# Moving a weight-tile store to the head of its pump slot, and one pump slot behind the softmax rescale, in an eight-core adaLN transformer layer

## What is computed

```python
h = _layernorm(x) * (1 + ca) + sa
x = x + ga * attn(h)      # k,q,v = h Wk', h Wq', h Wv'; ak = k Wa'
                          # alpha = softmax(q ak'); out = alpha (v Wb')
h = _layernorm(x) * (1 + cb) + sb
x = x + gb * ffn(h)       # two linears with LoRA, exact gelu between
# weights of the ffn:
scale = jnp.max(jnp.abs(w)) / qmax
wq = jnp.clip(jnp.round(w / scale), -qmax - 1, qmax) * scale
```

## Time and profile before

| | us |
|---|---|
| timed runs | 3199.82 and 3276.5, median 3238.16 |
| profiled execution | 3197.74 |
| its slowest core, first to last instruction (the span) | 3196.2 |
| fastest core of the same execution | 3181.2 |
| busy in the span: PE, DVE, ACT, POOL | 1727.2, 1033.1, 763.0, 436.4 |

### The profile page before, as it was taken

The page is one execution under the profiler, slowest core; times in us unless marked ns, Lnnn a source line. Parts: engine busy times, 40 slices in busy tenths (PEclk is TensorE's granted clock), DMA queues, the critical chain, the costliest instruction groups (busy, mean ns, idle before and its releaser), DMA issues.

```text
span 3196.2 us, 24948 instructions; the slowest of 8 cores (3181.2 to 3196.2 us)
## 1 busy us (share of the span) xinstructions
PE 1727.2 (54%) x7994; PEld 764.0 (24%) x7994; DVE 1033.1 (32%) x1773; ACT 763.0 (24%) x1325; POOL 436.4 (14%) x585
## 2 busy tenths in 40 slices
PE   4520040426666555455665555664525858858588
PEld 1110010112222222222232222232212323323233
DVE  3410333434444543444345434345411020110201
ACT  2310001032222231333233333233303122031220
POOL 0001122213333100111111122112200000000000
PEclk9855575758787767777777777777757979979799
DMA  4500424232222210111111222112241113112130
GB/s 141 177 6 5 138 84 132 76 115 70 68 70 69 73 57 30 56 69 70 60 56 66 75 67 69 60 57 70 69 166 53 60 46 99 51 56 65 47 99 27
DMA packets 92297, 233.40 MB, mean 73 GB/s; under 512 B 25380, under 2 KB 25509, under 8 KB 92152
## 3 DMA queue, kind: packets, MB, share of 16 engines
q1 hardware_dynamic: 65000, 160.33, 16.2%
q0 software_dynamic: 27168, 71.47, 6.7%
HBM read 193.85 MB, written 37.88 MB: 73 GB/s over the span
## 4 chain that ended last, share of the span: by engine, by line
PE 33%; DMA 24%; DVE 16%; issue 12%; ACT 10%; POOL 2%; SPq 1%; DVEq 1%; ACTq 0%; POOLq 0%
PE pO L1436 7%; PE pO L1198 5%; PE pE L1394 5%; PE pE L1101 5%; DMA wfcst<-wfcq_sc 4%; DMA amst<-wfc_in 4%; DMA amst<-wpj_in 4%; PE pE L1126 4%; ACT h_stage L729 3%; DVE qkf L960 2%; DMA wm<-wmod_in 2%; DMA q_stg<-q_sc 2%; DMA bfcT_sc<-lora 2%; DVE amx L621 2%; PE pE L742 1%
## 5 line engine op out<-in xcount | busy, mean ns | idle before, releaser
L1394 PE MATMUL pE<-h,wfcst 128*128 128x512 bf16 x1024 | 248.9, 387 | 54.2 <-DMA wfcst<-wfcq_sc 43.8
L936 POOL TENSOR_TENSOR qt<-qt,qkf 128x1024 f32<-128x1024 f32 x64 | 153.4, 2397 | 912.9 <-ACT qkf L930 898.5
L1436 PE MATMUL pO<-wpj_sb,hid 128*128 128x512 bf16 x1024 | 226.3, 379 | 16.1 <-DVE outb L1452 12.4
L1101 PE MATMUL pE<-ak_fm,q_stg 128*128 128x512 bf16 x512 | 144.0, 451 | 136.7 <-DMA q_stg<-q_sc 128.8
L621 DVE TENSOR_REDUCE amx<-amst 128x1 f32<-128x256 f32 x256 | 106.9, 418 | 183.6 <-DMA amst<-wfc_in 91.7
L1198 PE MATMUL pO<-u_tm,alphaT 128*128 128x512 bf16 x512 | 152.8, 472 | 22.0 <-DVE alphaT L1077 22.0
L930 ACT ACTIVATE qkf<-qki 128x512 f32<-128x512 int32 x128 | 80.5, 629 | 316.2 <-DVE qki L927 316.2
L1069 PE MATMUL pT<-idb,alphaA 128*128 128x128 bf16 x256 | 32.1, 305 | 220.7 <-DVE qbf L1011 135.6
L1409 ACT ACTIVATE hid<-pE,bfc_col 128x512 bf16<-128x512 f32 x128 | 88.0, 687 | 232.9 <-PE pE L1402 232.9
L742 PE MATMUL pE<-h_stage,wkaT 128*128 128x512 bf16 x512 | 125.3, 410 | 30.3 <-ACT h_stage L729 30.3
L1394 PEld LDWEIGHTS pE<-h,wfcst 128*128 128x128 bf16 x1024 | 92.1, 98 | 186.1 <-issue 98.3
(11 more groups left out here) (187 smaller groups left out, 2644.8 us busy)
## 6 DMA issues: line engine op xcount, KB each, us to landing
wfcst<-wfcq_sc SPq DMA_DIRECT2D x128, 256.0 KB, 2.6
wm<-wmod_in SPq DMA_DIRECT2D x32, 768.0 KB, 4.6
x_st<-x_in SPq DMA_DIRECT2D x48, 512.0 KB, 3.4
amst<-wfc_in POOLq DMA_DIRECT2D x128, 128.0 KB, 2.6
amst<-wpj_in POOLq DMA_DIRECT2D x128, 128.0 KB, 2.6
wst<-wfc_in SPq DMA_DIRECT2D x32, 512.0 KB, 3.5
wst<-wpj_in SPq DMA_DIRECT2D x32, 512.0 KB, 4.1
wfcq_sc<-qbf POOLq DMA_DIRECT2D x32, 256.0 KB, 2.3
```

Of the source, the lines that this page charges most:

```text
L936: t_dd = em("gpsimd", lambda e, qt=qt, qkf=qkf: e.tensor_tensor(out=qt[:], in0=qt[:], in1=qkf[:], op=OP.subtract), waits=[("s", t_kf)], in ...
L1101: t_eA = em("tensor", lambda e, oc=oc, jb=jb, p=p: e.matmul(out=s.pE[:, jb * 512:(jb + 1) * 512], lhsT=s.q_stage[p][:, oc * 128:(oc + 1) * ...
L1394: t_mm = em("tensor", lambda e, ic=ic, oc=oc, p=p, sl=sl: e.matmul(out=s.pE[:, sl * 512:(sl + 1) * 512], lhsT=wfcst[p][:, ic * 128:(ic + 1 ...
L1436: t_mm = em("tensor", lambda e, tt=tt, vc=vc, hc=hc: e.matmul(out=s.pO[:, vc * 512:(vc + 1) * 512], lhsT=hid[:, hc * 512 + tt * 128:hc * 5 ...
```

## The change

In `quant_slot` the call of the tile store moves from the end to the head. In `ph5` slot B moves from in front of the rescale to behind the last of the three one-column operations that follow it. No instruction is added or removed, and no buffer changes.

```diff
     def quant_slot(self, k):
+        if 0 <= k - 6 < 64:
+            self.quant_tile_store(k - 6)
         if 0 <= k - 1 < 64:
             self.quant_stageB1(k - 1)
             self.quant_stageB2(k - 1)
@@
         if k < 64:
             self.quant_stageA(k)
-        if 0 <= k - 6 < 64:
-            self.quant_tile_store(k - 6)
@@
             t_sA = em("scalar", lambda e: e.activation(
                 out=s.mcol[:, 4:5], in_=s.mcol[:, 3:4], func=AF.Exp),
                 waits=[("v", t_dc)], inc="s")
-            pump1()
             t_rs = em("vector", lambda e: e.tensor_scalar(
                 out=s.alphaA[:], in0=s.alphaA[:], scalar1=s.mcol[:, 4:5],
@@
             st["linv"] = t_linv
+            pump1()
             if ic > 0:
                 self._emit_pv(ic - 1, st, emit_trans, part=1)
             pump1()
```

## The result

The change costs 0.9%: ratio to the kernel before 1.0088, 95% interval 1.0073 to 1.0104 (medians 3229.66 and 3201.14 us over all runs). The profiled execution took 3225.37 us, its slowest core 3223.8, against 3197.74 and 3196.2. So the loss is 28 us, where the sum gave 8.

What follows compares the result with a forecast made beforehand. No single engine was taken as the bound, but a path passing between engines through slots B, C and A. The terms summed to +7.6 us on 3197.7, giving 3205; range 3160 to 3250, the forecast's own 3190 to 3241.

Steps and rivals of the forecast that it cites:

- the sum: Terms for slots A, B and C, iterations 0 and 15 and the tail: +7.6 us on the profiled 3197.7.
- rival 4: Slot B: x1b pair's second instruction holds off POOL's subtraction, 0.65 us in 15 iterations: +10, 3215; chance shared with forecast, 0.76.
- slot C: Its store, right behind the 512 KB x_sc store, up to 1.1 us late; 0.3 taken: +4.2, upper bound +11.
- landings of 3.4 us: Upper range term: stores land in 3.4 instead of 2.8 us: +15.
- the tail: Behind the loop, L960 and L965 now lie under the first of six serial stores' landing: -2.5 us.
- Slot A: Store at the head moves PV-0 by -0.32 us (wfcq, 8 times) or +0.18 (wpjq, 6 times): -2.6 and +1.1.
- today's distance of 3.47 holds after the move: Slots A and B: a wpjq_sc store lands 3.47 us after its copy L1011, as measured behind the loop.
- rival 3: Slots A and B: DVE's L920 and L927 hold up POOL's stores, 3.1 us in 29 slots: +91, 3296; chance 0.06.
- Slot B: Behind the rescale: L960 of slot C +0.32 us (iterations 1 to 8), +0.82 (9 to 14): +2.6 and +4.9.
- slot T: The store's copy falls into DVE's 2.01 us wait for ACT: cost nothing, or 0.60 us without that cover.
- Rival 1: Slots A and B: stores land before B3 needs them, PV-0 -0.72, L960 of slot C -0.08: -14, 3184; chance 0.08.
- Rival 2: Before PV-0: earlier transposes keep PE's clock up, gaining 2.6 us in each of 15 iterations: -39, 3166; chance 0.07.

Runs made afterwards that it cites:

- the run with the older wait: Changed kernel, but B3 (L978) waits only for stores of earlier slots, not its own: ratio 0.9934 to the kernel before, 21 us faster than it.
- the run with the later load: Changed kernel, but SP issues the weight load (L916) of slots A and B only when the slot's store has landed: ratio 0.9998 to the kernel before.
- edit 1 alone: Kernel before with only the store moved to the slot's head, slot B still in front of the rescale: ratio 1.0005.
- contiguous tiles: Changed kernel with second-matrix tiles stored as they lie (2 KB runs, not 256-byte), gather left to the feed-forward loads: ratio 1.0073 to the kernel before.
- edit 2 alone: Kernel before with only slot B moved behind the rescale, store still at the slot's end: ratio 0.9986.
- the best order of the slots: Kernel before with the store at the slot's head and B3 waiting only for older stores, slot B in front of the rescale: ratio 0.987.

## Why the prediction was right or wrong

It was right that the change makes no difference of 2%, and why it can't gain: B3's wait for its own slot's store takes up what the two moves free. That was the mechanism, and the run with the older wait shows it. What failed is the size of one term of the sum: the landing of a `wpjq_sc` store in slots A and B, taken as 3.47 us behind the copy and measured at 5.1 to 5.4 (more in iterations 10 and 15). So the forecast of 3205 was too low by 20 us or more, since the loss is 28 and not 8.

The time, 3229.7, lies even in the forecast's own range of 3190 to 3241, but partly by luck. Its upper bound had been raised by 10 us for rival 4, by 11 for slot C and by 15 for landings of 3.4 us. The first two came to nothing, and the third cost more than its 15 us. By parts of the sum, forecast and measured: the first nine intervals +2.8 and +0.4, the last six +7.8 and +25.0, from the last max-B to the last L1220 -0.5 and +4.5, the tail -2.5 and -2.0.

**Slot A.** Forecast PV-0 at 9.63 (first matrix) and 10.13 (second). Measured 9.6 to 10.1, and 11.7 to 12.4 but for iteration 10. The step that failed is "today's distance of 3.47 holds after the move": it was read behind the loop, where no load runs. I looked at what DVE would do beside the moved store (rival 3), and not at what SP would issue beside it, though its load of 512 KB follows L960 of the same slot. The order of issue gave it away: SP's load waits for L960, which follows the copy at once, so it comes 0.7 us behind the store in both slots. In quiet the 3.47 was right: it is what the run with the later load shows. The second half's 2.2 us were softened to +1.0 in an iteration, because PV-0 to max-B then takes 15.3 to 15.8 us and not 16.7.

**Slot B.** Forecast L960 of slot C at 16.99 and 17.49. Measured 16.98 to 17.17 in the first half (17.36 in iteration 1), right to 0.2, and 19.2 to 19.6 in the second, 1.8 later than the forecast: the same term again, 5.3 in place of 3.47. Over six iterations that is 2.6 x 6 = 16 us in place of 4.9. The rest of the argument held: the stall of L1160 is gone, and its 2.15 us reached nobody, because the ACT and POOL chain took over as the bound.

**Slot C and slot T.** Forecast +0.3 and nothing. Measured nothing: from L960 of slot C to that of slot T it is 9.62 us in nearly all iterations, as before, although B3 waits 1.2 to 1.5 us for its store there. The copy of slot T fell into DVE's wait for ACT. That slot C's slack covered it is shown by edit 1 alone, where it didn't.

**Iteration 10 and the end.** Iteration 10 lost almost 4 us more (interval 75.7 us, the next ones 71.7 to 72.0): POOL issued slot A's store 1.2 us late, which let SP's loads start ahead of it, and its first packet started only 4.3 us behind the issue; it landed 6.3 behind it. The late issue is there in each run with the store at the head, in the same iteration (with contiguous tiles it is in slot B of iteration 14). Its cause stays open. Behind the last max-B, +4.5 us up to the last L1220 stand against my -0.5, because slots B and C of iteration 15 wait for stores too; of the tail's -2.5 there came -2.0.

**Rivals.** Rival 1, that B3 isn't late, was wrong for this kernel, and right as a price: with the older wait the gain is 21 us, where it gave 14. Rival 2, the clock, asked for 7.1 us of PV-0 by the earlier transposes. With them PV-0 takes 9.3 to 9.9 us in the first half, as before (9.5 to 9.8), and 8.2 to 8.8 in iterations 11 to 15, where it also starts 2 us later. With the older wait it starts at the same offset nearly always and takes 8.4 to 8.9 us in eight of the iterations from 2 on and 9.8 to 9.9 in the other six; with edit 2 alone, whose transposes stand late, it is 8.3 and 8.4 twice. So the clock moves the time by about 1 us an iteration, and no run shows that the transposes are what moves it. Rival 3 named the right place and a wrong cause: the load and not DVE. Its threshold was also worked out wrongly: 57 us over 29 slots are 2.0 us a slot and not 1.7. Rival 4 did not come: the pair's second instruction (0.75 us) starts 0.1 us before slot B's subtraction in each iteration, and the subtraction still starts 0.14 behind the last cast and takes 2.35 us, as with nothing beside it (2.34).

## What to carry to other kernels

A wait on a counter that all DMAs of a kind share is fixed by where the call stands in the source. Before moving a store ahead of its waiters, freeze the count that they need: here that one wait is worth 49 us. Then ask what the other queues will issue in the microseconds behind the moved transfer. The landing time to use is the one read with that traffic beside it, not the one read in quiet. Here only the store whose packets started late, the one in short runs, met the load. And before tuning what stands on the path, look at the longest single wait of PE: taking the query load out from behind another load's wait gained 121 us, three times what the best order of the slots did.

## What the runs showed of the hardware

- A 256 KB store by POOL in 256-byte runs lands 2.8 to 2.9 us behind its issue alone, 4.5 to 4.9 when SP issues a 512 KB load 0.7 us behind it. The same 256 KB in 2 KB runs lands in 2.3 alone, and in 2.3 to 2.7 beside that load (once 3.4). Both have 80 packets of about 0.14 us; the first starts 1.49 and 1.1 us behind the issue, and the load's packets start 1.7 to 1.8 us behind it.
- PE's clock after an idle stretch came back after unequal times in this loop. In the run with both edits and the older wait PE stood idle for 5.55 us before PV-0 in two iterations in a row, and PV-0 began at 0.50 of full speed (1.2 GHz) in both. It got full speed (2.4 GHz) at 1381.64 in the one and at 1446.49 in the next:

```profile
1380.00:1381.00 1.00, 1.00 (x4) 0.43 (x3) 0.00 (x0) 0.00 (x0) 0.00 (x0) 0.50 0.00 0
1381.00:1382.00 1.00, 1.00 (x5) 0.35 (x4) 0.00 (x0) 0.00 (x0) 0.00 (x0) 0.68 0.00 0
...
1446.00:1447.00 1.00, 1.00 (x5) 0.35 (x3) 0.00 (x0) 0.00 (x0) 0.00 (x0) 0.75 0.00 0
1447.00:1448.00 1.00, 1.00 (x6) 0.49 (x5) 0.00 (x0) 0.00 (x0) 0.00 (x0) 1.00 0.00 0
```

  PV-0 started at 1375.79 and at 1443.27, and took 9.94 and 8.64 us for the same 32 matmuls. So the same order at the same offsets can differ by 1.3 us in one group of matmuls.
- A one-column DVE operation on two SBUF operands that began 0.31 us into a subtraction on POOL ended only with it: 2.30 us in place of 0.15, in 14 of 16 iterations. Moved to where POOL is idle, it takes 0.15 in all 16.
